# Four residual blocks on one core: all matrix products whose results nobody reads taken out

## The reference

```python
x = x + _L0_conv_ref(_gn(x), ...)   # group norm in 8 groups, 1x1 conv, relu, 1x1 conv
x = x + _L1_conv_ref(_gn(x), ...)   # four sweeps: down, up, right, left
x = x + _L2_conv_ref(_gn(x), ...)   # four sweeps again, without bias
x = x + _L3_conv_ref(_gn(x), ...)   # linear attention over all pixels, then 1x1 conv, gelu, 1x1 conv
...
def step(prev, row):                # one step of a sweep; prev is the row just made
    new = row + jax.nn.relu(_conv1d(prev, w, b))    # 9 taps along the row, 64 -> 64 channels
    return (new, new)
```

## The kernel before

| place | calls | products |
|---|---|---|
| statistics ahead of block 0 | WARM_STATS | 4 |
| ahead of ffn(0) | WARM_BLOCK | 5 |
| ahead of sweeps 0 and 4 | WARM_SWEEP | 4 each |
| after sweeps 1 and 5 (the turns) | WARM_TURN | 16 each |
| after the bias of block 3 | WARM_BLOCK | 5 |
| ahead of ffn(1) | WARM_BLOCK | 5 |

## Time and profile before

### The profile page before, as it was taken

How to read it: one execution, slowest core, us unless ns; L and a number is a source line. 1 busy time by engine, 2 the same in 40 slices (tenths; PEclk the granted TensorE clock), 3 DMA queues, 4 the chain that set the end, 5 groups by cost and what they waited for, 6 DMA issues and landing times. The chain is left out here.

```text
span 2610.4 us, 117000 instructions
## 1 busy us (share of the span) xinstructions
PE 2509.8 (96%) x46070; PEld 2417.0 (93%) x46070; DVE 1813.5 (69%) x5782; ACT 1236.6 (47%) x2705; POOL 352.7 (14%) x547
## 2 busy tenths in 40 slices
PE   1999999999999999999899999999999999998998
PEld 1389999999999999999899999999999999997885
DVE  7866666666666666677666666666666666777986
ACT  0866664222233333377666642222333333675877
POOL 1620000000000000066000000000000000653545
PEclk9999999999999999999999999999999999998999
DMA  7810001222450000087600012223600000430006
GB/s 270 219 45 0 0 0 36 61 60 60 91 54 0 0 4 1 0 258 161 190 8 0 0 29 60 60 60 88 66 0 0 0 0 0 129 97 2 4 4 258
DMA packets 323834, 155.07 MB, mean 59 GB/s; under 512 B 155169, under 2 KB 319650, under 8 KB 319650
## 3 DMA queue, kind: packets, MB, share of 16 engines
q1 hardware_dynamic: 321600, 153.41, 22.9%
q10 hardware_dynamic: 2146, 0.53, 0.1%
HBM read 70.00 MB, written 50.33 MB: 46 GB/s over the span
## 5 line engine op out<-in xcount | busy, mean ns | idle before, releaser
L870 PE MATMUL banks<-x_row,w_taps 128*64 128x124 f32 (+2 forms) x40640 | 2200.4, 270 | 5.4 <-DVE x_row L1114 3.1
L870 PEld LDWEIGHTS banks<-x_row,w_taps 128*64 128x64 f32 x40640 | 2198.8, 135 | 7.1 <-issue 6.1
L1123 DVE SCALAR_TENSOR_TENSOR x_row<-banks,sweep_nbias,biased_row 128x128 f32<-128x128 f32 x2032 | 712.9, 351 | 717.1 <-PE banks L870 695.1
L666 ACT ACTIVATE biased_row<-state,sweep_bias 128x256 f32 (+1 forms) x762 | 512.2, 673 | 1038.9 <-DVE state L1126 605.7
L662 ACT ACTIVATE biased_row<-state,aff,gn_a 128x64 f32 (+1 forms) x1016 | 364.2, 429 | 184.4 <-DVE state L1132 184.4
L1126 DVE SCALAR_TENSOR_TENSOR state<-banks,sweep_nbias,biased_row 128x128 f32 (+1 forms) x1016 | 443.0, 436 | 0.0
L550 POOL TENSOR_TENSOR state<-state,stripe_a 128x256 f32<-128x256 f32 x96 | 66.9, 733 | 1982.3 <-DVE state L1126 1962.0
L1132 DVE SCALAR_TENSOR_TENSOR state<-banks,sweep_nbias,biased_row 128x64 f32 (+1 forms) x1016 | 236.9, 275 | 0.1
L1132 DVE SCALAR_TENSOR_TENSOR turn_ring<-banks,sweep_nbias,biased_row 128x64 f32<-128x64 f32 x1016 | 236.7, 274 | 0.0
L843 PE MATMUL banks<-res,ffn_w 64*64 64x512 f32 x512 | 112.3, 597 | 6.1 <-ACT res L599 5.2
L832 PE MATMUL banks<-state,ffn_s 64*64 64x512 f32 x512 | 106.8, 598 | 0.2 <-DVE ffn_s L1285 0.2
(11 more groups left out here) (138 smaller groups left out, 903.3 us busy)
## 6 DMA issues: line engine op xcount, KB each, us to landing
state<-turn_ring SPq DMA_DIRECT2D x512, 64.0 KB, 1.9
resid<-state SPq DMA_DIRECT2D x94, 256.0 KB, 3.6
state<-x_in SPq DMA_DIRECT2D x16, 1024.0 KB, 20.7
stripe_a<-resid SPq DMA_DIRECT2D x32, 512.0 KB, 5.3
stripe_b<-resid SPq DMA_DIRECT2D x32, 512.0 KB, 5.4
out_y<-state SPq DMA_DIRECT2D x16, 1024.0 KB, 4.1
res<-resid SPq DMA_DIRECT2D x32, 256.0 KB, 7.3
resid<-state SPq DMA_DIRECT2D x16, 512.0 KB, 6.7
```

What stands on the lines that cost most here:

```text
L666: nc.scalar.activation(as_cells(n, biased_row[:, k, :, :]), cells(n, slice(0, B), i, k, g), ACT.Identity, bias=sweep_bias[:, n:n + 1]).the ...
L870: last = nc.tensor.matmul(out_ps[blk, :, lo:hi], w_taps[:, n % 2, s, blk], x_row[c][src][:, :, s + lo:s + hi], start=at == 0, stop=at == T ...
L1123: nc.vector.scalar_tensor_tensor(x_row[c][par][:, :, 2:2 + HALF], ps, nb, br, ALU.max, ALU.add).then_inc(row_ready[c], 1)
```

## The change

`keep_warm` and its eight calls are deleted, and the four constants with them. Nothing else is changed: the other engines' programs are the same row by row, and PE's is the same without the 59 products.

```diff
-    WARM_STATS, WARM_BLOCK, WARM_SWEEP, WARM_TURN = 4, 5, 4, 16
...
-            def keep_warm(products):
-
-                for _ in range(products):
-                    nc.tensor.matmul(bank[5][:, 0:P], gmats[:, 0, :], ones[:].bitcast(F32), start=True, stop=True)
-
...
             stat_product(1, gn_t[:, 2, :])
-            keep_warm(WARM_STATS)
...
             nc.tensor.matmul(bank[7][:, 0:B], ffn1_w[:], aff[:, 1, :], start=True, stop=True).then_inc(small_product_done, 1)
-            keep_warm(WARM_BLOCK)
...
                 if n % 4 == 0:
                     stat_product(0, mv[:, :, 0])
                     stat_product(0, gn_t[:, 3, :])
-                    keep_warm(WARM_SWEEP)
                 sweep(n)
-                if n % 4 == 1:
-                    keep_warm(WARM_TURN)
...
             nc.tensor.matmul(bank[7][0:C, 0:B], wq_t[:], gn_c[0:C, :], start=True, stop=True).then_inc(small_product_done, 1)
-            keep_warm(WARM_BLOCK)
...
                              stop=True).then_inc(small_product_done, 1)
-            keep_warm(WARM_BLOCK)
             ffn(1)
```

## The result

Without the 59 products the kernel takes 2617.3 us (median of 18 runs, 2615.38 to 2618.58), before 2612.02 (18 runs of the same job, 2609.82 to 2613.18): ratio 1.0020, interval 1.0013 to 1.0027, so 5.3 us slower (3.4 to 7.1). The forecast was 2617.7 and +6.7.

A forecast was written before the change was run, and what follows sets the result against it. PE bounds the sweeps and ffn(1), DVE ffn(0). Terms 4.4 + 0 + 0.6 + 1.4 + 0 + 0.3 + 0 = +6.7 us on the median 2610.96 gave 2617.7, range 2614.0 to 2621.2.

The forecast's parts named there:

- The turns: Ahead of sweeps 2 and 6: without the 16 products each, the sweep starts at the half clock level; +4.4 us (3.2 to 5.5).
- ffn(0): Ahead of ffn(0): up starts earlier but at half level, DVE's first add comes later, delaying sweep 0; +1.4 us (0.8 to 1.8).
- Sweep 0: Four products ahead of sweep 0: it already starts low, so removal costs nothing; 0 us (-1.15 to 0).
- Sweep 4: Four products ahead of sweep 4: low time of 3.2 us becomes 4.4; +0.6 us (0 to 1.15).
- Block 3 after its bias: Five products: first tile starts 0.66 us earlier, cancelled by half-speed work; 0 us (-0.6 to +0.6).
- ffn(1): Five products ahead of ffn(1): up runs at half, mostly covered by ACT's work; +0.3 us (0 to +0.8).
- my price: Starts at the half level: where PE is the bound, half the low time is lost; 2.2 us (1.6 to 2.8).
- The dip: First tiles of block 3: the later clock fall, 3.4 us at 0.50, may or may not recur; 0 us (-1.7 to 0).
- the clock that holds: Rival: the clock stays up through the holes, so only two delays by products go; 2609.7 us, chance 0.05.
- Only the turns pay: Rival: elsewhere the clock returns when it does today; 4.4 at the turns, +4.9 in all, 2615.9 us, chance 0.20.
- Every start long: Rival: all low times are like sweep 0's 5.5 us; +9.9, 2620.8 us, chance 0.15.
- separate draws: All places: low times vary independently, so the sum stays nearer its centre within +0.6 to +9.9 us.

## Why the prediction was right

It was right in kind, in place and within its range: 2617.3 against 2617.7 forecast, and by the size of the change +5.3 against +6.7. By its own steps:

- **The turns.** Forecast +4.4 (3.2 to 5.5). In the profile 1.94 + 1.88 = 3.8; the kernel without the turns' products alone is 3.7 slower by its runs, and its trace has 2.26 + 1.94 = 4.2 there. The mechanism is shown: PEclk 0.50 behind the uncovered hole, the loss half of the low time. The size of the low time was a little off, 3.9 to 4.7 us in the two kernels' profiles where I took 4.4 as the middle of two starts. (The 42 and 23 instructions that I read as the pace are not starts: those that reach into a window count too. The starts in 2 us are 37 and 19, and 37 agree with 55 ns each.)
- **ffn(0).** Forecast +1.4 (0.8 to 1.8) on DVE's first add. Measured 0.7 in the changed kernel (0.9 in its second profile), 1.7 and 1.8 in two others with the same edit; the means of all profiles with and without the products are 1.2 apart. The step that the delay goes through whole held (79.0, 79.0, 79.3 us from add to ACT's start in three kernels, before 79.0).
- **Sweep 0.** Forecast 0, down to -1.15 if the low time should come out shorter. It did: 4.0 us instead of 5.5, -0.7 in the profile. I had called that a draw, but it came in all four profiles of kernels without these four products: sweeps 0 and 1 take 550.48 to 551.28 us there, and 551.44 to 551.66 in the six profiles that have just the four. So the cost of nothing that I gave the removal is the weak step here: it goes with a gain of 0.2 to 1.1 us. Why is not shown; a later start alone doesn't do it, since the kernel without ffn(0)'s products begins sweep 0 2.3 us later than before and has 551.48.
- **Sweep 4.** Forecast +0.6 (0 to 1.15); +0.33 in the changed kernel's profile (low 3.9 us), +1.1 with only these products gone, -0.1 with all but the turns' gone. That is the term's range; that the products cause any of it is not shown.
- **Block 3 after its bias.** Forecast 0. The first tile starts 0.63 us earlier, forecast 0.66, and the kernel without block 3's products shows no difference in all. But the reason I gave, half-speed work cancelling the earlier start, was not the one: of the 0.63 the last tile still has 0.54, and what cancels it in the kernel without block 3's products is ffn(1), which takes 0.7 more. The clock stayed at half for 12.4 us from the first tile, far outside my 3.2 to 5.5:

```profile
2388.39 0.74 PE L905 MATMUL banks<-bias_rows,picks 64*128 64x448 f32 x2 [1.70 <-DVE bias_rows L1216]
...
2390.00:2400.00 10.00, 10.00 (x133) 7.38 (x125) 4.23 (x7) 5.85 (x9) 1.90 (x4) 0.50 0.01 2
...
2401.36 0.64 PE L927 MATMUL banks<-res 64*64 64x64 f32 x32
```

By my price, the 5.9 us that this is longer than the kernel before's 6.5 would have cost 3. They cost 0.1 (143.77 against 143.68 in the table above). One place where the kernel before loses what its faster first tiles win is a wait for the normalisation chain of DVE ahead of the first Gram product:

```profile
2396.44 0.69 PE L939 MATMUL banks<-res 64*64 64x64 f32 x32 [1.26 <-DVE res L1261]
```

That row and the half level behind it are gone in the changed kernel, whose first Gram product waits for nothing. The step that failed is the price, half of every low microsecond: PE sets the pace among the first tiles only in part. By the table the first 6 us cost 0.25 to 0.3 each and the rest nothing, and the kernel before, with its dip, already paid 1.9 us of the 2.0 that the changed kernel pays. The dip that I had put at 0 to -1.7 is gone, but in a longer low stretch, so nothing was won; alone, a dip of 3.4 us costs 1.1 (142.85 against 141.75). That the sum came out as forecast is luck in this term.

- **ffn(1).** Forecast +0.3. Its first down starts 4.10 us after its first up, before 3.86, and from there to the end it is 59.96 against 59.79: +0.4. In the two other kernels without its products it is 0.7, still within its range up to 0.8.
- **Not in the sum.** In the chain between the last Gram product and ffn(1) the clock came back for a while, so that L951 took 1.16 us (its row of before had 2.09): 0.9 us of the profile's -1.07 in block 3. The second profile shows the same. It is no effect of a step that I can name.

The sum of the profile is +3.3, that of the medians +5.3. Three terms of the profile lie on the favourable side (ffn(0) 0.7, sweep 0 -0.7, the chain -0.9), and its execution is one of the fastest of the 18; but the timed runs leave no trace, and their granted clock, 0.985 in all 18, is too coarse to tell (0.001 of it is 2.6 us of PE's time), so where the others spend their 2 us is open. That it is these same terms is likely by the kernels above, where ffn(0) cost 1.8 and sweep 4 1.1, and not shown.

Of the rivals, the clock that holds is wrong: it fell at both turns in every profile without the products. "Only the turns pay" is not refuted as a whole: its +4.9 lies inside the interval of the measurement (3.4 to 7.1). It had 0.8 at ffn(0), where 0.7 to 1.8 were measured, and nothing at sweep 4, which is undecided; it is wrong at ffn(1), where it had nothing and 0.4 to 0.7 were measured. "Every start long" met no turn; the longest low time, in block 3, cost no more than half of it had cost before. The rule of the Trainium skill (TensorE: Matmul & The Clock Gate, "What's actually happening") that the number of slow products differs from run to run does not show in the two profiles of each kernel, which agree within 0.3 us at the sweeps. It does in the timed runs of the kernel before, whose granted clock goes from 0.988 to 0.991 and their time with it. That the places of one run are separate draws was my step and not the rule's, and no run here shows it.

## What to carry to other kernels

Work whose result nobody reads can hold up the clock: before taking it out, look at the level of PEclk behind each hole that it fills, and multiply the low time by a half only where PE is the engine that sets the pace there. Here 16 products in a wait of 5.5 us were worth about 2 us each time, eight of them a quarter to a third of that, and the ten in block 3 nothing in sum: five delayed its first tile by 0.6, five saved ffn(1) 0.4 to 0.7. If such filling pays, fill the whole wait, small gaps included: with gaps of 0.7 to 2.1 us left between the fillers no gain was clear of none, with them closed it was 5. And for a place worth a microsecond take several profiles before saying what it costs: the profile of one kernel had sweep 4 at +1.1, that of another with the same four products gone at -0.1.

## What was not expected of the hardware

- The clock can fall after the dense work has begun: with a hole of 3.3 us sweep 2 ran at full for 1.4 us and then fell, for 3.4 us; and once with a hole of only 2.0 us, where 1.5 us never brought it down in the profiles here.
- The return can take long though PE works without a hole: 3.9 to 4.7 us behind the turns in sweeps, but 12.4 us among the tiles of block 3 in the changed kernel, where PE was busy 10.00 of 10 us. It is not the work alone: in the two profiles of the kernel before the first return came 3.1 and 9.9 us after the first tile, and 1.6 in the kernel without the turns' products.
- The low times at the sweeps repeat between two profiles of one kernel (4.05 and 4.1 us at the first turn, 5.5 and 5.8 at sweep 0), and yet the kernel before's timed runs spread over 4 us (2609.17 to 2613.47) with granted clocks from 0.988 to 0.991.
